# Expert part: batch 3 turned into the other output banks, the first output ahead of its logits, the gate biases one unit later

## What is computed

```python
mla_out = ao @ o_w + o_b
probs = jax.nn.softmax(mla_out @ router_w + router_b, axis=-1)
topw, topi = jax.lax.top_k(probs, TOPK)                       # TOPK = 2 of E = 8
topw = topw / (topw.sum(-1, keepdims=True) + 1e-08)
combine = jnp.sum(jax.nn.one_hot(topi, E, dtype=probs.dtype) * topw[..., None], axis=-2)
h1 = jnp.einsum('bsd,edf->ebsf', mla_out, w1) + b1[:, None, None, :]
h1 = jax.nn.gelu(h1, approximate=False)
h2 = jnp.einsum('ebsf,efd->ebsd', h1, w2) + b2[:, None, None, :]
moe_out = jnp.einsum('bse,ebsd->bsd', combine, h2)
return hs + 0.3 * moe_out
```

## Time and profile before

| | us |
|---|---|
| median of 3 runs | 1686.81 |
| lowest and highest | 1686.24, 1693.86 |
| the profiled execution | 1692.87 |
| its span in the profile | 1690.9 |
| TensorE busy in it | 1620.2 (96%) |
| VectorE busy | 1437.7 (85%) |
| ScalarE busy | 1207.2 (71%) |

### The profile page before, as it was taken

The page is one execution under the profiler, slowest core; times in us unless marked ns, Lnnn a source line. Parts: engine busy times, 40 slices in busy tenths (PEclk is TensorE's granted clock), DMA queues, the critical chain, the costliest instruction groups (busy, mean ns, idle before and its releaser), DMA issues.

```text
span 1690.9 us, 38163 instructions
## 1 busy us (share of the span) xinstructions
PE 1620.2 (96%) x14822; PEld 713.5 (42%) x14822; DVE 1437.7 (85%) x2093; ACT 1207.2 (71%) x1205; POOL 456.0 (27%) x564
## 2 busy tenths in 40 slices
PE   4999999999999999998999999999999999989996
PEld 2444444444444444445233333333332332466774
DVE  6677778888888888897999999999999999478888
ACT  2776666666667666654887888788878888656776
POOL 2311112332322333332234232323332331220004
PEclk9999999999999999998999999999999999989998
DMA  5311101111011001011012000200030000000001
GB/s 153 71 37 38 37 20 39 38 37 37 36 37 37 34 24 38 22 32 32 14 39 49 11 13 16 48 14 13 17 73 22 14 16 14 1 1 14 13 12 50
DMA packets 46754, 53.39 MB, mean 32 GB/s; under 512 B 9309, under 2 KB 33581, under 8 KB 46638
## 3 DMA queue, kind: packets, MB, share of 16 engines
q1 hardware_dynamic: 45588, 50.06, 10.3%
q10 hardware_dynamic: 1050, 1.73, 0.4%
HBM read 15.59 MB, written 10.49 MB: 15 GB/s over the span
## 4 chain that ended last, share of the span: by engine, by line
PE 86%; DVE 6%; ACT 3%; issue 2%; POOL 1%; ACTq 0%; POOLq 0%; DVEq 0%
PE psum L1807 15%; PE psum L567 15%; PE psum L548 11%; PE psum L1792 9%; PE psum L1818 7%; PE psum L512 5%; PE psum L1448 5%; PE psum L1413 4%; PE psum L585 3%; DVE arena L2268 3%; PE psum L605 2%; PE psum L530 1%; ACT arena L2036 1%; PE psum L532 1%; PE psum L531 1%
## 5 line engine op out<-in xcount | busy, mean ns | idle before, releaser
L2268 DVE TENSOR_REDUCE arena<-psum 128x2 f32<-128x1024 f32 x490 | 585.6, 1220 | 39.0 <-PE psum L1818 33.0
L2036 ACT ACTIVATE arena<-psum 128x1024 f32<-128x1024 f32 x512 | 523.8, 1025 | 132.0 <-PE psum L1792 118.0
L721 ACT ACTIVATE arena<-psum 128x2048 f32<-128x2048 f32 (+1 forms) x160 | 274.0, 1712 | 231.6 <-PE psum L548 231.4
L1807 PE MATMUL psum<-arena 128*32 128x256 f32 x4096 | 327.9, 392 | 0.7
L813 POOL TENSOR_SCALAR_AFFINE_SELECT arena<-arena 128x512 f32<-128x512 f32 (+1 forms) x160 | 151.7, 966 | 521.9 <-ACT arena L721 521.9
L567 PE MATMUL psum<-arena,hs 128*64 128x512 f32 (+3 forms) x1536 | 283.0, 496 | 0.1
L548 PE MATMUL psum<-arena 64*128 64x512 f16 (+3 forms) x2304 | 216.3, 325 | 3.8 <-DVE arena L859 3.4
L1792 PE MATMUL psum<-arena 32*128 32x512 bf16 x1024 | 198.9, 385 | 3.7 <-DVE arena L2268 3.1
L1818 PE MATMUL psum<-arena 32*128 32x512 bf16 x980 | 189.1, 382 | 5.9 <-ACT arena L2036 2.4
L859 DVE TENSOR_TENSOR arena<-arena 128x1024 f16<-128x1024 f32 x64 | 80.3, 1255 | 101.0 <-ACT arena L700 101.0
L567 PEld LDWEIGHTS psum<-arena,hs 128*64 128x64 f32 x1536 | 95.9, 136 | 141.4 <-issue 125.2
(11 more groups left out here) (221 smaller groups left out, 2112.7 us busy)
## 6 DMA issues: line engine op xcount, KB each, us to landing
arena<-arena SPq DMA_DIRECT2D x30, 512.0 KB, 2.9
arena<-arena SPq DMA_DIRECT2D x46, 128.0 KB, 2.2
arena<-latent_q SPq DMA_DIRECT2D x64, 64.0 KB, 2.0
arena<-latent_k SPq DMA_DIRECT2D x64, 64.0 KB, 2.0
arena<-arena SPq DMA_DIRECT2D x60, 64.0 KB, 2.4
X<-in_L_attn_states SPq DMA_DIRECT2D x4, 512.0 KB, 6.2
latent_q<-arena SPq DMA_DIRECT2D x16, 96.0 KB, 2.2
latent_k<-arena SPq DMA_DIRECT2D x16, 96.0 KB, 2.3
```

Source lines behind the costliest of these rows:

```text
L721: nc.scalar.activation(probs[g], SC[:, :, 0:WIDTH[g]], ACT.Exp, scale=DH ** -0.5).then_inc(exp_done, 1)
L1807: last = nc.tensor.matmul(OT[ROWS * c:ROWS * (c + 1), h * HALF // 2:(h + 1) * HALF // 2], v_cols[par][:, kt, 2 * pr + i, :], e_probs[u % 4 ...
L2036: nc.scalar.activation(e_probs[u % 4], src, ACT.Exp, scale=KD ** -0.5).then_inc(e_done, 1)
L2268: nc.vector.tensor_reduce(half_tops[:, kh, qt, 2 * pr:2 * pr + 2], src.rearrange("p (i c) -> p i c", i=2), AX.X, ALU.max).then_inc(top_don ...
```

## The change

- The last batch is transposed into `YP[1]` instead of `YP[0]`, when bank 6 has been read by ScalarE (`raw_copied`), and its logits go to the first columns of `YP[1]` once VectorE has copied the turned tokens out.
- `output(0)` stands ahead of `route_last` on TensorE. It waits for the early logits (`lg_ready` 6) and no more for the copies of batch 3. `output(1)` waits for the last logits, `lg_ready` 7, as before.
- On VectorE `add(0, 0)` stands ahead of `take_last_logits`, and `softmax(1)` to `finish_weights(1)` stand after `add(0, 2)` instead of after `add(0, 0)`. On ScalarE `exponentials(1)` stands after unit 3 instead of after unit 2.
- `BIASES_AT` goes from 2 to 3: the weights are turned after the hidden pass of unit 4, and the biases follow the outputs 3 to 6 instead of 2 to 5. ScalarE copies the turned weights after unit 4 instead of after unit 3. `HP[0]` is free for them when unit 4's first half has been read (`gelu_done` 9).
- On TensorE the experts 2 and 3 are written out, since `output(7)` has a wait of its own now, and the loop covers 4 to 7 instead of 2 to 7.

```diff
@@ -1255,7 +1255,7 @@
         HP = [bank(0, 2), bank(2, 2)]
         YP = [bank(4, 2), bank(6, 2)]
         TURNED = YP[0]
-        LOGITS, LAST_LOGITS = [bank(n)[:, 0:GH * E] for n in (4, 5)], SPARE[:, 0:T * E]
+        LOGITS, LAST_LOGITS = [bank(n)[:, 0:GH * E] for n in (4, 5)], YP[1][:, 0:T * E]
         READY_AT, READY_STEP = 12, 6
 
         mT_ps, mT_ready, mhi_ready, mlo_ready = sem("mT_ps"), sem("mT_ready"), sem("mhi_ready"), sem("mlo_ready")
@@ -1273,7 +1273,7 @@
         last_out_ready = sem("last_out_ready")
         N4 = E * B
         LOWS_SHARED = 3
-        BIASES_AT = 2
+        BIASES_AT = 3
         HT = T // 2
 
 
@@ -1326,7 +1326,7 @@
 
         def take_turned(dve, b, h):
 
-            src = TURNED[:, h * HALF:(h + 1) * HALF]
+            src = (TURNED if b < EARLY else YP[1])[:, h * HALF:(h + 1) * HALF]
             dve.wait_ge(mT_ps, 2 * b + h + 1)
             nc.vector.tensor_copy(mT_b[b][:, h * HALF:(h + 1) * HALF], src).then_inc(mT_ready, 1)
             nc.vector.tensor_copy(half_batch(mT[:, 0, :], b, h), src).then_inc(mhi_ready, 1)
@@ -1384,14 +1384,15 @@
             def turn_last():
 
                 pe.wait_ge(proj_added, 2 * B)
-                pe.wait_ge(lg_ready, 2 * EARLY)
+                pe.wait_ge(raw_copied, 2 * N2)
                 for t in range(T):
-                    last = nc.tensor.transpose(TURNED[:, t * P:(t + 1) * P], acc[:, EARLY * T + t, :], ident[:, :])
+                    last = nc.tensor.transpose(YP[1][:, t * P:(t + 1) * P], acc[:, EARLY * T + t, :], ident[:, :])
                     if t % GH == GH - 1:
                         last.then_inc(mT_ps, 1)
 
             def route_last():
                 pe.wait_ge(mT_ready, 2 * B)
+                pe.wait_ge(mhi_ready, 2 * B)
                 for t in range(T):
                     last = nc.tensor.matmul(LAST_LOGITS[:, t * E:(t + 1) * E], mT_b[EARLY][:, t * P:(t + 1) * P],
                                             w_router[:, :], start=True, stop=True, skip_group_check=True)
@@ -1402,7 +1403,7 @@
                 n = B * e + b
                 if isinstance(e, int) and e == 0 and b == 0:
                     pe.wait_ge(e_done, ITEMS * N2)
-                elif c == 0 and isinstance(n, int) and n == B:
+                elif c == 0 and isinstance(n, int) and n == B + 1:
                     pe.wait_ge(cT_ready, 1)
                 else:
                     pe.wait_ge(gelu_done, FC * (n - 1) + c + 1)
@@ -1430,10 +1431,8 @@
 
                 pe.wait_ge(act_split, FC * (n + 1))
                 if isinstance(n, int) and n == 0:
-                    pe.wait_ge(mT_ready, 2 * B)
-                    pe.wait_ge(mhi_ready, 2 * B)
+                    pe.wait_ge(lg_ready, 2 * EARLY)
                 elif isinstance(n, int) and n == 1:
-                    pe.wait_ge(raw_copied, 2 * N2)
                     pe.wait_ge(lg_ready, 2 * EARLY + 1)
                 elif isinstance(n, int) and BIASES_AT < n <= BIASES_AT + B:
                     pe.wait_ge(b2_added, n - BIASES_AT)
@@ -1452,7 +1451,7 @@
             def turn_weights():
 
                 pe.wait_ge(cw_ready, 2)
-                pe.wait_ge(gelu_done, FC * B - 1)
+                pe.wait_ge(gelu_done, FC * B + 1)
                 for k in range(2):
                     last = nc.tensor.transpose(HP[0][:, k * P:(k + 1) * P],
                                                c_tok[:, k * TC:(k + 1) * TC, :].rearrange("p t e -> p (t e)"), ident[:, :])
@@ -1467,7 +1466,7 @@
                 k, at = b * T // TC, b * T % TC
                 for half in range(2):
                     first = at + half * T // 2
-                    last = nc.tensor.matmul(YP[(b + 1) % 2][:, half * HALF:(half + 1) * HALF], cT[:, k * P:(k + 1) * P],
+                    last = nc.tensor.matmul(YP[(BIASES_AT + b + 1) % 2][:, half * HALF:(half + 1) * HALF], cT[:, k * P:(k + 1) * P],
                                             b2_diag[:, first:first + T // 2, :].rearrange("p t d -> p (t d)"),
                                             start=True, stop=True)
                 last.then_inc(b2_done, 1)
@@ -1475,10 +1474,11 @@
             def expert(e, par, biases=False):
                 for b in range(B):
                     hidden(e, par, b)
+                    if biases and b == 0:
+                        turn_weights()
                     output(B * e + b - 1, par if b > 0 else 1 - par, (b - 1) % 2)
-                    if biases and b < B - 1:
-                        bias(b + 1)
-
+                    if biases:
+                        bias(b)
 
             hidden_inputs(0, 0, 0)
             hidden_half(0, 0, 0, 0)
@@ -1492,16 +1492,16 @@
             turn_last()
             hidden_inputs(0, 0, 2)
             hidden_half(0, 0, 2, 0)
+            output(0, 0, 0)
             route_last()
-            output(0, 0, 0)
             hidden_half(0, 0, 2, 1)
             output(1, 0, 1)
             hidden(0, 0, 3)
-            turn_weights()
             output(2, 0, 0)
-            bias(0)
             expert(1, 1, biases=True)
-            with pe.Fori(1, E // 2) as k:
+            for par in range(2):
+                expert(2 + par, par)
+            with pe.Fori(2, E // 2) as k:
                 for par in range(2):
                     expert(2 * k + par, par)
             pe.wait_ge(gelu_done, FC * (N4 - 1) + 1)
@@ -1537,11 +1537,12 @@
             unit_half(0, 0, 1)
             unit(0, 1)
             unit(0, 2)
+            unit(0, 3)
             exponentials(act, 1)
-            unit(0, 3)
+            unit(1, 0)
             act.wait_ge(cT_ps, 1)
             nc.scalar.copy(cT, HP[0][:, 0:2 * P]).then_inc(cT_ready, 1)
-            for b in range(B):
+            for b in range(1, B):
                 unit(1, b)
             with act.Fori(2, E) as e:
                 for b in range(B):
@@ -1624,7 +1625,7 @@
                 dve.wait_ge(b2_done, b + 1)
                 dve.wait_ge(y_added, b + 1)
                 v = batch(hs, b)
-                nc.vector.tensor_tensor(v, YP[(b + 1) % 2].rearrange("p (t d) -> p t d", t=T), v, ALU.add
+                nc.vector.tensor_tensor(v, YP[(BIASES_AT + b + 1) % 2].rearrange("p (t d) -> p t d", t=T), v, ALU.add
                                         ).then_inc(b2_added, 1)
 
             def finish(b):
@@ -1654,14 +1655,15 @@
             for h in range(2):
                 take_inputs(EARLY, h)
             finish_weights(0)
+            add(0, 0)
             take_last_logits()
             centre(1)
-            add(0, 0)
-            softmax(1)
-            find_largest(1)
-            finish_weights(1)
             for e in range(2):
                 for b in range(1 if e == 0 else 0, B):
+                    if e == 0 and b == EARLY:
+                        softmax(1)
+                        find_largest(1)
+                        finish_weights(1)
                     if B * e + b >= LOWS_SHARED - 1:
                         low_act(dve, nc.vector, B * e + b + 1, (b + 1) % 2)
                     add(e, b)
```

## The result

| | before | after |
|---|---|---|
| median of 20 runs each | 1692.87 | 1697.50 |
| lowest and highest | 1684.73, 1697.21 | 1694.16, 1703.96 |
| the profiled execution | 1692.87 | 1701.67 |
| its span | 1690.9 | 1699.8 |

The ratio of after to before is 1.0047, with a 95% interval of 1.0034 to 1.0060: the changed kernel is slower by about 8.0 us (5.8 to 10.2). The two medians lie only 4.63 apart, because they fall into different groups of the runs (next paragraph). The forecast was +5.4. The time itself, 1697.50, lies in the range, but partly for a reason that isn't mine: over 20 runs the median of before is 1692.87 and not the 1686.81 of its first three, on which I had put the sum.

The account below looks back on a forecast made before the run. A chain over VectorE was taken to set the end of the expert part's start, before TensorE is packed. Delays of 3.66 to hidden(5) plus 1.78 for biases made +5.4 on 1686.81, so 1692.2, range 1687 to 1699.5.

Parts of the forecast that it names:

- Step 1: TensorE, output(0) ahead of the logits: the 1.28 us wait and slow output(0) vanish, TensorE 2.1 us or more ahead.
- Step 2: VectorE, add(0, 0) ahead of the last logits: the early gain is lost and output(1) starts 1.45 us later.
- Step 3: TensorE's clock behind the wait ahead of output(1): low, so it takes 5.12 instead of 2.68, +2.44 us.
- Step 4: VectorE's chain to the turned weights ends at 1519.10; TensorE idles 6.2 us and output(3) starts +1.15 in all.
- Step 5: TensorE, output(3) behind the 6.2 us wait: low clock again, +2.44; hidden(5) starts +3.66 in all.
- Step 6: Biases from hidden(5) on: three left instead of two, +1.78 us, making the steady part 5.4 later.
- Step 7: TensorE, experts 2 and 3 written out of the loop: a taken branch costs nothing here, so no gain.
- The sum: Whole kernel: +5.4 us added to a before median of 1686.81 gives 1692.2.
- A: Rival: TensorE's clock holds through one or both waits, +3.0 (1689.8) or +0.6 (1687.4); chance 0.12.
- B: Rival: clearly slower, 1697.5, if median before-runs lack the low stretch at 1490, or 1698.3 with the 784 stretch after; 0.27.
- C: Rival: VectorE doesn't hold output(1), so it and all behind it come 4 us earlier, 1682.8; chance 0.04.
- D: Rival: the order makes no difference, VectorE's chain being hidden by work counted twice, 1686.8; chance 0.04.

Follow-up runs that it names:

- experiment 5: Changed kernel with last logits taken within finish_weights(0) and GpSimd's low part of unit 2 waiting for the first gate weights; ratio to before 1.0005, median 1690.42.
- Experiment 1: Changed kernel with one more wait: GpSimd starts the low part of unit 2 only after finish_weights(0); ratio to before 1.0032, median 1694.94.
- experiment 2: Kernel before, with GpSimd repeating a subtraction of batch 3's low part twice, to be busy beside finish_weights(0); one run, 1691.69.
- experiment 3: Changed kernel with take_last_logits put back ahead of add(0, 0) on VectorE; ratio to before 1.0029, median 1693.72.
- Experiment 6: Changed kernel with 40 and 24 unread matmuls filling TensorE's two long waits; ratio to before 1.0026, median 1696.78.
- experiment 7: Kernel before with only output(0) ahead of the logits and the banks this needs; biases and VectorE's order kept; ratio to before 1.0019, median 1693.21.
- experiment 8: Changed kernel with logits within finish_weights(0), GpSimd's low part of unit 2 later, exp, second softmax and second weights earlier; ratio to before 0.9978, median 1686.11.
- experiment 4: Changed kernel with take_last_logits and centre(1) moved within finish_weights(0), behind its searches; ratio to before 1.0010, median 1689.86.

## Why the forecast was right and wrong

**Step 1** was right. `output(0)` at 1488.45 (my 1488.05, plus the 0.41) in 2.84, no wait ahead of the logits, and half 2/1 over at about 1494.2.

**Step 2 failed, by 3.60 of the 8.49.** Its sentence was that `finish_weights(0)` "is neither shortened nor begun earlier". True, but it is lengthened: two of its steps grew by 3.56 together. I had moved the adds and the logits on VectorE, and had not followed what else `output(0)` sets free: ScalarE's unit 2, and behind it GpSimd's two instructions, the one engine that I never set against VectorE. The earlier trace rows hold no GpSimd row. The trace of before had the sign of it: the cast L1592 took 0.71, and ended at 1494.03, when GpSimd's L1284 ended at 1493.99; with GpSimd idle it takes 0.18 (experiment 5). Experiment 1 removes the holds and gives my numbers back, experiment 2 makes them in the old kernel.

**Step 3**: mechanism right, its size too high. `output(1)` took 4.57 start to start, not 5.12, with the clock at 0.56. The end of the low clock lay within it. Experiments 3 and 5 show the same for `output(3)`, 3.94 and 4.04. Experiment 6 makes both slow outputs go away with the waits.

**Steps 4, 5 and 6** were right to 0.07 each: hidden(3) to the turning 14.02 (forecast 14.08), the turning to hidden(5) 7.52 (7.45), hidden(5) to hidden(9) 27.64 (27.65). The wait ahead of the turning was 5.99, released by VectorE, forecast 6.2; `output(3)` took 5.33 at a clock of 0.50.

**Step 7** cost nothing that shows: 142.09 from hidden(9) to the end in both kernels.

**The sum.** 3.60 - 0.55 = 3.05 turns +5.44 into +8.49. I had also called 8.4 us about the least that a measurement of this kernel can tell from none, and gave 0.70 to a change smaller than that; 20 runs of each show 8.0 with an interval of 5.8 to 10.2, a loss clear of the noise. The second term of the sum that failed is the base: I took the median of three runs for the kernel's, but its runs fall into two groups 7 us apart. The stretch at 784 at half clock belongs to it: T0 is 1475.6 to 1477.8 in the five traces with the clock at 1.00 there (experiments 1 to 5) and 1481.9 to 1483.6 in the five with 0.50 to 0.56 (before, after, experiments 6, 7 and 8), and the program text up to T0 is the same in all ten. So traces with it are 4.1 to 7.9 us later at T0, where I had "about six", and within the five that have it T0 still varies by 1.66, which covers the 0.41 between before and after. The profiled executions of the experiments 1, 3, 4 and 5 also lie in the lower part of their kernels' runs, and those of before, after and the experiments 6 and 7 in the upper. The window at 784 of experiment 1, and of after:

```profile
784.00:797.00 13.00, 11.00 (x94) 5.71 (x90) 9.72 (x23) 7.88 (x8) 1.31 (x6) 1.00 0.36 74
```

```profile
784.00:797.00 13.00, 13.00 (x59) 7.49 (x56) 6.17 (x21) 5.25 (x5) 1.31 (x6) 0.51 0.38 87
```

94 matmuls are done in the first and 59 in the second, in the same 13 us. By its T0 experiment 8 fits too: 1482.02, with 0.50. But its run, 1685.73, lies in the middle of 1680.2 to 1691.3, so those runs don't fall into two groups as plainly. Since each kernel has one trace, it is made likely and not shown that this stretch alone sets the groups of the runs.

**The rivals.** A: the clock held through neither wait. B named 1697.5, and the median is 1697.50, but neither of its ways to it shows: the one further trace of the old order, experiment 2, has the low clock behind its wait of 1.27 as well, and the median run after is one of the lower group. The number fits by chance. C's condition was made in experiment 4, and its price, "all behind it 4 us earlier", was wrong: what `output(1)` gained, `output(2)` waited. D: 8.49 says no.

**What stays open.** What chooses between the two groups, why the same output costs more behind one wait than behind another of the same length, and how the 8.49 divides over VectorE's order and the later biases, which were not tried apart.

## What to carry to other kernels

When an operation is moved forward, follow everything that it sets free on every engine, and set the new times of GpSimd's instructions beside VectorE's steps that read two operands from SBUF (here a cast with one as well): such a step lasts until GpSimd's instruction ends, and the trace shows that as its duration and not as a wait. A gain at one output is worth nothing while a chain over another engine meets TensorE one unit later; here the chain to the second weights had to be shortened as well, and only then did both long waits and both slow outputs go (2.56 was the longest wait left). Take more than three runs before a median carries a sum.

## What the runs showed of the hardware

- A VectorE step with two SBUF operands, 0.20 or 0.36 us alone, takes up to 2.06 to 2.17 beside a GpSimd step of 2.12, and a cast of 128x48 from SBUF 0.71 to 2.13 instead of 0.18. In experiment 2 each GpSimd instruction held one VectorE step, four in a row. Adds with a PSUM operand are unmoved (2.15 to 2.16 for 8), and so is a reciprocal of 128x24, which reads one operand (0.30 in experiment 4, within GpSimd's second step, and 0.30 in experiment 8, with GpSimd idle).
- Behind a wait of 4.2 to 9.6 us the same output took between 3.94 and 5.33 instead of 2.84; the length of the wait didn't order them (6.00 gave 3.94 and 5.99 gave 5.33). Waits of 2.36 to 2.57 gave 2.84, 2.85, 4.29 and 4.46 (experiments 7, 8, 2 and 5), and the 1.28 of the kernel before 5.17, the 1.27 of experiment 2 4.37, in both behind the logits.
